# S4D filter convolution and LoRA layer on one core: corner products of each head in hi/lo parts

## What is computed

```python
result = einsum('bsd,od->bso', x, base_weight) + base_bias
lora_out = einsum('bsr,bor->bso', einsum('bsd,brd->bsr', x, A[ids]), B[ids])
x = x + result + lora_out
y = irfft(rfft(x, n=2 * L) * rfft(K, n=2 * L))[..., :L] + x * D
x = x + y * (arange(L) < length)
```

## Time and profile before

| | |
|---|---|
| Runs | 1257.44, 1257.80, 1258.69 us; median 1257.8 |
| Profiled execution, first to last instruction | 1257.1 us, 0.7 us below that median |
| TensorE busy | 1242.0 us, 99% |
| Weight loads busy | 1067.6 us, 85% |
| DVE busy | 719.9 us, 57% |
| ACT busy | 349.2 us, 28% |
| POOL busy | 191.7 us, 15% |
| DMA | 190.31 MB, mean 151 GB/s |

### The profile page before, as it was taken

The page is one execution under the profiler, slowest core; times in us unless marked ns, Lnnn a source line. Parts: engine busy times, 40 slices in busy tenths (PEclk is TensorE's granted clock), DMA queues, the critical chain, the costliest instruction groups (busy, mean ns, idle before and its releaser), DMA issues.

```text
span 1257.1 us, 15957 instructions
## 1 busy us (share of the span) xinstructions
PE 1242.0 (99%) x6408; PEld 1067.6 (85%) x6408; DVE 719.9 (57%) x883; ACT 349.2 (28%) x494; POOL 191.7 (15%) x73
## 2 busy tenths in 40 slices
PE   7999999999999999999999999999999999999998
PEld 6788888888888888888888888878888888888887
DVE  5765545555455554334143241437888888888877
ACT  4332232322322222112032020213333333333332
POOL 1000000000000000000000000004444444444443
PEclk9999999999999999999999999999999999999999
DMA  6441340423405234052240431516876677757872
GB/s 200 144 168 66 104 161 8 168 73 98 164 6 168 77 93 165 5 168 108 61 167 5 163 142 26 197 57 224 268 274 236 214 261 276 252 202 258 267 262 101
DMA packets 117934, 190.31 MB, mean 151 GB/s; under 512 B 9508, under 2 KB 91621, under 8 KB 111845
## 3 DMA queue, kind: packets, MB, share of 16 engines
q1 hardware_dynamic: 117860, 189.30, 44.7%
HBM read 121.87 MB, written 67.40 MB: 151 GB/s over the span
## 4 chain that ended last, share of the span: by engine, by line
PE 97%; DVE 1%; DMA 1%; ACT 0%; issue 0%; SPq 0%; DVEq 0%
PE acc L889 55%; PE acc L959 30%; PE acc L871 5%; PE acc L902 5%; PE acc L949 2%; DMA w_raw<-w_t 0%; PE acc L911 0%; DMA x_raw<-x_t 0%; DVE u_lo L526 0%; DVE x_sb L571 0%; ACT w_hi L391 0%; DVE t_lo L526 0%; DVE w_lo L526 0%; ACT hh L391 0%; DVE y_sb L800 0%
## 5 line engine op out<-in xcount | busy, mean ns | idle before, releaser
L889 PE MATMUL acc<-x_hi,w_hi 128*128 128x512 f32 x1024 | 403.2, 394 | 9.0 <-DVE x_lo L526 6.9
L889 PE MATMUL acc<-x_lo,w_hi 128*128 128x512 f32 x1024 | 401.4, 392 | 0.0
L889 PE MATMUL acc<-x_hi,w_lo 128*128 128x512 f32 x1024 | 400.1, 391 | 0.0
L857 POOL TENSOR_TENSOR out_sb<-y_sb,u_raw 128x1024 f32<-128x1024 f32 x63 | 187.6, 2979 | 1058.0 <-DMA u_raw<-x_scratch 852.8
L571 DVE SCALAR_TENSOR_TENSOR x_sb<-acc,bias_sb,x_raw 128x512 f32<-128x512 f32 x128 | 93.5, 747 | 319.6 <-PE acc L902 319.5
L959 PE MATMUL acc<-u_hi,t_hi 128*128 128x512 f32 (+2 forms) x648 | 242.4, 374 | 2.3 <-DVE u_hi L822 1.7
L889 PEld LDWEIGHTS acc<-x_hi,w_hi 128*128 128x128 f32 x1024 | 193.7, 189 | 47.0 <-issue 6.9
L959 PE MATMUL acc<-u_hi,t_lo 128*128 128x512 f32 (+2 forms) x648 | 232.7, 359 | 0.0
L959 PE MATMUL acc<-u_lo,t_hi 128*128 128x512 f32 (+2 forms) x648 | 231.5, 357 | 0.0
L889 PEld LDWEIGHTS acc<-x_hi,w_lo 128*128 128x128 f32 x1024 | 193.3, 189 | 41.5
L889 PEld LDWEIGHTS acc<-x_lo,w_hi 128*128 128x128 f32 x1024 | 193.9, 189 | 35.4
(11 more groups left out here) (124 smaller groups left out, 857.0 us busy)
## 6 DMA issues: line engine op xcount, KB each, us to landing
x_scratch<-x_sb SPq DMA_DIRECT2D x16, 2048.0 KB, 7.3
t_raw<-filter_scratch SPq DMA_DIRECT2D x16, 2048.0 KB, 15.3
out<-out_sb SPq DMA_DIRECT2D x63, 512.0 KB, 3.7
x_raw<-x_t SPq DMA_DIRECT2D x15, 2048.0 KB, 13.4
u_raw<-x_scratch SPq DMA_DIRECT2D x15, 2048.0 KB, 10.2
a_raw<-lora_a SPq DMA_DIRECT2D x128, 64.0 KB, 4.1
b_raw<-lora_b SPq DMA_DIRECT2D x128, 64.0 KB, 4.0
w_raw<-w_t SPq DMA_DIRECT2D x7, 512.0 KB, 5.4
```

The lines of the kernel that those rows point to most:

```text
L857: pool.tensor_tensor(out_sb[h % OUT_BUFS][:, :, :].rearrange(view, b=GH), y_sb[h % 2][:, :, :].rearrange(view, b=GH), u_source(h, 0, n_gro ...
L889: mm = pe.matmul(acc[:, n % O_BANKS, :], w, m, start=k == 0 and i == 0, stop=False)
```

## The change

The corner of every head becomes three matmuls of 128 columns of t_hi, t_lo, u_hi and u_lo, in the loop's common path. The fp32 matmul, t_full, its copy on ACT, its semaphore and the waits for it go. So does the widening in heads 0 to 3. ACT and DVE split all 8 tiles of t in every head. A removed run of empty lines at the file's head is left out here.

```diff
@@ -150,7 +129,6 @@
     assert cursor[0] <= x_raw_at
     cursor[0] = x_split_at
     OUT_BUFS = 3
-    t_full = [place(f"t_full{i}", [P, 2, P], F32) for i in range(2)]
     y_sb = [place(f"y_sb{i}", [P, NT, batch], F32) for i in range(2)]
     out_sb = [place(f"out_sb{i}", [P, NT, batch], F32) for i in range(OUT_BUFS)]
 
@@ -184,7 +162,6 @@
                                                       ["wlo", "xlo", "alo", "blo", "hlo", "ulo", "tlo"])
     c_w0hi, c_w0lo = sem("c_w0hi"), sem("c_w0lo")
     c_uhi_early = sem("c_uhi_early")
-    c_tfull = sem("c_tfull")
     c_hlow = sem("c_hlow")
 
     c_last = sem("c_last")
@@ -214,10 +191,6 @@
     def y_bank(h):
 
         return (O_BANKS + 2 * h) % 8
-
-    def split_tiles(h):
-
-        return NT if h < HQ else NT - 1
 
     def w_loaded(t):
 
@@ -295,8 +268,6 @@
             def load_t(q):
                 if q >= 2:
                     sp.wait_ge(c_tlo, HQ * (q - 1))
-                    if q >= 3:
-                        sp.wait_ge(c_tfull, HQ * (q - 2))
                 src = bass.AP(k_d.tensor, q * HQ * KROW + KPAD - (P - 1), [[1, P], [KROW, HQ], [1, L]])
                 sp.dma_start(t_raw[q % 2][:, :, :, :].rearrange("p h t n -> p h (t n)"), src).then_inc(ld_t[q % 2], 16)
 
@@ -484,11 +455,7 @@
             def split_t(h):
                 q, r = divmod(h, HQ)
                 act.wait_ge(ld_t[q % 2], 16 * (q // 2 + 1))
-                nt = split_tiles(h)
-                copy(t_hi[h % 2][:, 0:nt, :], reversed_cols(t_raw[q % 2][:, r, 0:nt, :])).then_inc(c_thi, 1)
-                if h >= HQ:
-                    copy(t_full[h % 2][:, :, :],
-                         reversed_cols(t_raw[q % 2][:, r, NT // 2 - 1::NT // 2, :])).then_inc(c_tfull, 1)
+                copy(t_hi[h % 2][:, :, :], reversed_cols(t_raw[q % 2][:, r, :, :])).then_inc(c_thi, 1)
 
             def split_u_early(h):
 
@@ -728,9 +695,8 @@
             def split_t(h):
                 q, r = divmod(h, HQ)
                 dve.wait_ge(c_thi, h + 1)
-                nt = split_tiles(h)
-                minus_hi(t_lo[h % 2][:, 0:nt, :], reversed_cols(t_raw[q % 2][:, r, 0:nt, :]),
-                         t_hi[h % 2][:, 0:nt, :]).then_inc(c_tlo, 1)
+                minus_hi(t_lo[h % 2][:, :, :], reversed_cols(t_raw[q % 2][:, r, :, :]),
+                         t_hi[h % 2][:, :, :]).then_inc(c_tlo, 1)
 
             def split_u_early(h):
                 dve.wait_ge(c_uhi_early, h + 1)
@@ -932,8 +898,6 @@
                 if h == 2:
                     pe.wait_ge(c_x1, NT * n_groups)
                 pe.wait_ge(c_tlo, h + 1)
-                if h >= HQ:
-                    pe.wait_ge(c_tfull, h - HQ + 1)
                 pe.wait_ge(c_ulo, h + 1 + min(h + 1, HQ))
                 if h >= 4:
                     pe.wait_ge(c_y, h - 3)
@@ -944,13 +908,6 @@
                         first = max(d, HALF * half)
                         end = HALF * (half + 1)
                         last = d == blocks[-1]
-                        if end - first == 1 and h >= HQ:
-
-                            mm = pe.matmul(bank[:, (HALF - 1) * batch:], t_full[h % 2][:, half, :],
-                                           u_raw[h // HQ % 2][:, :, h % HQ, 0, :], start=False, stop=last)
-                            continue
-                        if end - first == 1:
-                            first -= 1
                         src = slice(first - d + 1, end - d + 1)
                         cols = slice((first - HALF * half) * batch, (end - HALF * half) * batch)
                         t_pair = (t_hi[h % 2][:, d, :], t_lo[h % 2][:, d, :])
```

## The result

The changed kernel takes 1270.23 us (median of 4 runs, 1269.37 to 1272.19); the kernel before, with one run more, 1258.24. The ratio is 1.0099, 95% interval 1.0084 to 1.0113: about 12 us slower. The forecast was 1271.1. The profiled execution of the changed kernel is the one of 1272.19 us, the slowest of the four.

A forecast was written before the change was run, and what follows sets the result against it. TensorE's stream was taken as the bound: 384 narrow products at 0.1125 us (43.2) less 29.9 for what they replace gave +13.3 us on a 1257.1 us span, so 1270.4, plus 0.7 for 1271.1 us; range 1266 to 1316.

The forecast's parts named there:

- The bound: Second stage: from head 4 on nothing but TensorE releases TensorE, so each microsecond added to its stream lengthens the kernel.
- The price of a narrow product: Each 128-column hi/lo corner product on TensorE is paced by its weight load: 0.1125 us, bounds 0.065 and 0.225.
- Rival A: Corner products: loads hide under wide neighbours, only moving columns count, 0.065 us each; -4.9 us, 1252.9; chance 0.06.
- C: Rival: hi/lo corner products each cost what the fp32 corner does, 0.225 us; +56.5 us, 1314.3; chance 0.24.
- D: Rival: load and columns add up in corner products, 0.168 us; +34.6 us, 1292.4; chance 0.13, including anything between it and forecast.
- B: Rival: near no change, corner products at 0.071 to 0.084 us, 1257 to 1260; chance 0.03.
- E: Rival: corner products stay 256 columns wide at 0.12 us; +16.2 us, 1274.0; shares 0.54 with the load-paced forecast.
- The price of the corner it replaces: Each fp32 corner on TensorE, heads 4 to 63, costs 0.225 us; 120 removed save 27.0 us.
- Both ways: Two derivations of the fp32 corner's price, from a whole later head and from head 3, each subtracting 5.90 us.
- the second way: Head 3's 6.69 us, less 0.07 restart and six widened corner products at 0.12, leaves 5.90 us without corners.
- The first heads: Heads 0 to 3: 24 corner products narrow from 256 to 128 columns, -0.2 us, which might not arrive.
- The other engines: ACT +0.11 us, DVE +0.16 per head, covered by TensorE; without cover, tenths of a microsecond at some 14 group switches.

The follow-up runs named there:

- e5: Changed kernel without its corner products, so one output tile per half lacks them: 1240.14 us, ratio 0.9860 to the kernel before.
- e10: Changed kernel with each corner's three products done twice, six in all: 1314.49 us, ratio 1.0454 to the kernel before.
- e2: Changed kernel with 64 instead of 128 moving columns in the corner products: 1268.88 us, ratio 1.0090 to the kernel before.
- e3: Changed kernel with 64 of 128 weight columns in the corner products, placed ahead of the 256-column products: 1257.17 us, ratio 0.9993 to the kernel before.
- e1: Changed kernel with its corner products widened to 256 columns in all heads: 1272.56 us, ratio 1.0113 to the kernel before.
- e4: Kernel before with all 8 tiles of t split on ACT and DVE in every head, fp32 corner and its copy kept: 1259.04 us, ratio 1.0012.
- e6: Changed kernel with two of the three corner products, lo weights by hi columns left out: 1255.22 us, ratio 0.9983 to the kernel before.
- e7: Changed kernel with each half's three corner products issued singly between wide products: 1270.75 us, ratio 1.0103 to the kernel before.
- e8: Kernel before with 64 instead of 128 moving columns in its fp32 corner, heads 4 to 63: 1259.09 us, ratio 1.0008.
- e12: Kernel before with 64 of 128 weight columns in its fp32 corner, placed ahead of the 256-column products: 1293.88 us, ratio 1.0290.
- e9: Changed kernel with corners of 192 moving columns, 64 zeros ahead of the tile: 1271.36 us, ratio 1.0111 to the kernel before.

## Why the prediction was right

**The bound.** TensorE's stream alone sets the second stage. Heads have one length, nothing but the two early waits releases TensorE, and the sum over all heads, 12.0 less 0.3 us, is the measured change. Right.

**The price of a narrow product.** Forecast 0.1125 us, by way of the loads' distance; measured 0.115 (e5, e10). The load as its cause is shown by e2 and e3 together: half the columns change next to nothing, half the weight columns give the forecast saving. Rival A fell with e2, C and D with the head of 6.56 us, B with the time, E with the groups of 128 columns.

**The price of the corner it replaces.** This is the term that was mis-sized: "a corner now costs 0.225 us" was 0.245. Both ways to it shared the base of 5.90 us a head, and that was 0.03 high: the second way took it from the widened corners of head 3 at 0.12 a product and a restart of 0.07, where e1 gives 0.122 and head 1, without a restart, takes 6.60 us instead of 6.62. The chain and the starts around a pair, 0.14 us to the next record and 0.31 instead of 0.23 behind that the earlier trace rows, give 0.22. The other 0.02 falls on the products behind these, and the prediction's own trace shows it. Head 4 has fp32 corners but stands behind the hi/lo corner of head 3. It begins at 871.50, and the next head at

```profile
877.76 0.48 PE L959 MATMUL acc<-u_hi,t_hi 128*128 128x512 f32 x1
```

That is 6.26 us, where all later heads take 6.36. So 0.10 us of a corner falls behind it, 0.08 of it on the first product, and a corner is 0.14 + 0.10 = 0.24. Each head so grew by 0.69 - 0.49 = 0.20 us instead of 0.225, 12.0 in place of 13.5 over 60 heads.

**The first heads.** Forecast -0.2 us, measured: from the stage's start to head 4's start 871.50 - 844.18 = 27.32 before and 872.82 - 845.82 = 27.00 after, -0.3.

**The other engines.** No cost in the changed kernel, right, and for the reason given: the longer head gives more than the split takes. The size of the cover was wrong (0.28 us, of which 0.26 was hand-over; e4). At a switch of groups u_lo now ends at 1028.62 + 1.21 = 1029.83, and TensorE begins at 1030.26, 0.43 us later:

```profile
1028.62 1.21 DVE L493 TENSOR_TENSOR u_lo<-u_raw,u_hi 128x1024 fp32r<-128x1024 f32 x1
...
1030.26 0.44 PE L916 MATMUL acc<-u_hi,t_hi 128*128 128x512 f32 x1
```

The corner ahead of it is a hi/lo one now, where the hand-over takes 0.10 to 0.15 us (e5). In e6 a distance of 0.21 at the switches cost nothing. So a real cover of some 0.3 us stands there, where there was 0.02. DVE's subtraction of t takes 1215 ns at the median, forecast 1239, and up to 3457 beside POOL:

```profile
L493 DVE TENSOR_TENSOR t_lo<-t_raw,t_hi x64: 1162/1215/3457, 838.7 to 1254.6; 128x1024 fp32r<-128x1024 f32 x64
```

The same split beside the old corner cost 1.2 us (e4). The prediction's "tenths of a microsecond each" holds for that case.

**The total.** The forecast of the span, 1270.4, met 1270.5 by luck: the sum was 1.6 us too high (13.3 against 11.7), and the profiled execution lost 1.6 us more than the one before to the early clock. Against the medians the change was forecast 1.3 us too large (13.3 against 12.0), and the time only 0.9 us too high, because the median of the kernel before rose by 0.4 with its fourth run. The "0.7 around the span" was misread: it is the distance from one execution's span to the median of other runs. The changed kernel's profiled run is 1272.19 us for a span of 1270.5, so 1.7 lies around it. As the same 0.7 was put on both sides, it cost the forecast nothing.

**The figure of the Trainium skill.** The 81 ns per 128-column matmul of "TensorE: Matmul & The Clock Gate", section "Back-to-back issue gap", would have given +1.2 us. The runs don't agree: measured are 115 ns for fp32r operands with 128 weight columns, in a head, in the middle of a corner, and in a run of six.

**Is there a faster version?** None was found. Spreading the narrow products gains nothing (e7), and of the two ways tried to compute a corner in full the fp32 product has two loads, the hi/lo form three. Operands of other types were not tried.

## What to carry to other kernels

Count weight loads before columns: here an fp32r matmul with 128 weight columns cost 0.114 to 0.122 us at 64 to 256 moving columns, about its weight load, and an fp32 matmul cost what two loads do, a hi/lo triple three. Take the price of an instruction from the length of a whole repeating unit with and without it, as the distances between single records moved by up to 0.08 us at a change of type or width. And take the hand-over off the distance between the producer's end and the consumer's start before calling it cover: here it took 0.26 us behind an fp32 corner and 0.10 to 0.15 behind hi/lo products.

## What was not expected of the hardware

- A wait of TensorE of 0.10 us per switch (e4) shows in no wait view, since the record of the corner outlasts it; only the head's length shows it.
- TensorE's start came 0.26 us after DVE's end behind an fp32 corner (e4; 0.25 at the one late head of e8), and 0.10 to 0.15 us behind hi/lo products (e5, and head 3 of either kernel). Open.
- The fp32 matmul with 64 weight columns lost the overlap of its loads and cost 0.55 us instead of 0.245 (e12), while fp32r matmuls of the same width and place got cheaper (e3). Open.
- The price of an fp32r product rises slowly, 0.114 to 0.122 us from 64 to 256 columns, and has no sharp edge at which the columns take over (e2, e9, e1).
- Up to 3 us of a run's time hang on whether the granted clock falls to the lower level once in the first 50 us: the second stage starts at 842.2 to 843.0 us in the nine traces without a fall there, at 844.1 to 845.1 in the three where the first 100 us have a mean of 0.98, and at 845.8 and 846.1 in the two with 0.97.
